# VectorE computes one of the four exponential banks in 88 of 1024 units of an attention layer

## The reference

```python
x = x + attn(_layernorm(x))          # in: (4, 2048, 256)
x = x + ffn(_layernorm(x))
# attn
qkv = einsum('bse,fe->bsf', x, in_proj_weight) + in_proj_bias
scores = einsum('bhqd,bhkd->bhqk', q * scale, k)
scores = where((j <= i) & (j >= i - 16), -inf, scores)
ctx = einsum('bhqk,bhkd->bhqd', softmax(scores), v)
out = einsum('bse,fe->bsf', ctx, out_proj_weight) + out_proj_bias
# ffn
h = tanh(((x @ weight) @ aux_weight1) @ aux_weight2 + bias)
```

## Time and profile before

| | us |
|---|---|
| median of 3 runs (2016.45 to 2018.87) | 2017.15 |
| the profiled execution's own time | 2016.49 |
| its span, first to last instruction | 2014.8 |
| ACT busy | 1927.0 (96%) |
| PE busy | 1822.5 (90%) |
| DVE busy | 703.0 (35%) |
| POOL busy | 153.7 (8%) |

### The profile page before, as it was taken

How to read it: one execution, slowest core, us unless ns; L and a number is a source line. 1 busy time by engine, 2 the same in 40 slices (tenths; PEclk the granted TensorE clock), 3 DMA queues, 4 the chain that set the end, 5 groups by cost and what they waited for, 6 DMA issues and landing times.

```text
span 2014.8 us, 100136 instructions
## 1 busy us (share of the span) xinstructions
PE 1822.5 (90%) x46728; PEld 752.1 (37%) x46728; DVE 703.0 (35%) x1415; ACT 1927.0 (96%) x2113; POOL 153.7 (8%) x178
## 2 busy tenths in 40 slices
PE   7799999999999999999999999999998978888895
PEld 4333343343434334343343434334342323223232
DVE  6233343433444343343434334343432212121123
ACT  4599999999999999999999999999999999999994
POOL 2000000101010010101101000010100000000001
PEclk9899999999999999999999999999999999999998
DMA  4400111101231110102221111211022010000101
GB/s 132 140 26 27 47 33 55 42 22 47 65 93 33 53 43 17 58 25 64 63 63 52 28 57 30 59 38 42 21 67 66 22 42 22 25 30 12 42 14 44
DMA packets 93448, 93.76 MB, mean 47 GB/s; under 512 B 17562, under 2 KB 84570, under 8 KB 93026
## 3 DMA queue, kind: packets, MB, share of 16 engines
q1 hardware_dynamic: 92772, 87.05, 14.8%
q10 hardware_dynamic: 256, 0.26, 0.1%
HBM read 52.56 MB, written 25.72 MB: 39 GB/s over the span
## 4 chain that ended last, share of the span: by engine, by line
ACT 54%; issue 29%; PE 15%; DMA 1%; DVE 1%; SPq 1%; POOL 0%; DVEq 0%
ACT probs L1220 53%; PE outs L1287 7%; PE scores L1268 4%; PE ps_qk L487 2%; ACT s_pre L1212 1%; PE ps_v L504 1%; PE spare L1370 1%; SPq L155 0%; PE spare L1315 0%; PE spare L1326 0%; PE ps_turn L457 0%; DMA inverse<-row_inverse 0%; DMA xin<-in_x 0%; PE spare L1302 0%; PE scores L1475 0%
## 5 line engine op out<-in xcount | busy, mean ns | idle before, releaser
L1220 ACT ACTIVATE probs<-scores 128x1024 f32<-128x1024 f32 x2048 | 1887.3, 1112 | 22.5 <-PE scores L1268 20.4
L1287 PE MATMUL outs<-probs,vs 64*32 64x512 f32 x16384 | 1077.1, 590 | 0.0
L1268 PE MATMUL scores<-qs,ks 49*32 49x512 f16 x16384 | 840.2, 383 | 158.8 <-ACT probs L1220 143.8
L1268 PEld LDWEIGHTS scores<-qs,ks 49*32 49x32 f16 x16384 | 233.8, 89 | 1079.2 <-ACT probs L1220 1044.2
L1287 PEld LDWEIGHTS outs<-probs,vs 64*32 64x32 f32 x16384 | 302.3, 106 | 35.7 <-issue 10.5
L886 DVE TENSOR_TENSOR probs<-probs,allowed 128x320 f32<-128x320 f32 (+2 forms) x280 | 147.5, 530 | 337.6 <-ACT probs L1220 337.4
L1326 PE MATMUL spare<-s_xt,w_qkv 64*32 64x256 f32 x3072 | 120.7, 375 | 0.0
L828 POOL TENSOR_TENSOR s_squares<-s_qk_f 128x512 bf16<-128x512 f32 x48 | 61.3, 1278 | 384.5 <-DVE s_qk_f L957 384.5
L822 POOL TENSOR_TENSOR s_x<-s_x,bias_o 128x1024 f32<-128x1024 f32 x16 | 38.2, 2385 | 573.7 <-DMA s_x<-in_x 573.7
L954 DVE TENSOR_SCALAR s_qk_f<-spare,bias_qk 128x512 f32<-128x512 f32 x48 | 36.1, 751 | 129.8 <-PE spare L1326 129.8
L1016 DVE TENSOR_TENSOR s_x<-s_x,spare 128x512 f32<-128x512 f32 x30 | 20.7, 688 | 171.5 <-PE spare L1326 171.5
(11 more groups left out here) (119 smaller groups left out, 786.6 us busy)
## 6 DMA issues: line engine op xcount, KB each, us to landing
qs<-q_parts SPq DMA_DIRECT2D x192, 64.0 KB
ks<-k_parts SPq DMA_DIRECT2D x192, 64.0 KB
inverse<-row_inverse SPq DMA_DIRECT2D x32, 256.0 KB
s_x<-in_x SPq DMA_DIRECT2D x16, 512.0 KB, 5.6
ctx_in<-raw SPq DMA_DIRECT2D x248, 32.0 KB, 2.0
out<-s_pre SPq DMA_DIRECT2D x15, 512.0 KB, 3.5
s_xin<-in_x SPq DMA_DIRECT2D x12, 512.0 KB, 6.3
q_parts<-s_parts SPq DMA_DIRECT2D x24, 256.0 KB, 2.3
```

Source lines behind the costliest of these rows:

```text
L1220: act.activation(probs[:, u % RING, 2 * slot:2 * slot + 2].rearrange("p c q -> p (c q)"), scores[:, 2 * slot:2 * slot + 2].rearrange("p c ...
L1268: last = pe.matmul(scores[cols, 2 * slot + e], ks[rows, group, keys], qs[rows, group], start=True, stop=True)
L1287: last = pe.matmul(outs[32 * c:32 * c + 32, side], vs[keys, at:at + 2 * HD], probs[keys, u % RING, c], start=(i == 0), stop=(i == KBLOCKS ...
```

## The change

In 88 units, ACT computes only three of the four banks (slot 1 becomes one instruction of 512 columns), and DVE computes `exp` of the fourth bank (bank 3) with a polynomial: `share(u, stage)`, in four stages at the positions u + 1 to u + 4. Stage 1 reads the bank from PSUM and signals `taken`, after which PE may write the bank again; the last instruction of stage 4 writes `probs` and signals `shared_done`. The units are r = 11, 27, 32, 42, 60 in steps 0 to 11, and r = 1, 7, 12, 27, 33, 38, 57 in steps 12 to 15. The weighing lags by a constant 5 units (before: 4 for i = 4 to 12 of a pass, 3 for i = 14 to 31 and the first three, two weighings at i = 13, none at i = 3). The ring has 7 units. At the position after a shared unit the weighing is cut into two halves of 256 columns, one on each side of `score(u, 1)`. Some pieces are moved by a position, `evacuate` goes from r = 3 and 35 to 5 and 37, `invert` from r = 8 and 40 to 10 and 42, and the fp16 high part of a projected query or key moves from `take_qk` to `split_low`, a position later.

```diff
-RING = 8
+RING = 7
+LAG = 5
-TURN_AT = (7, 8, 9, 10)
-QK_AT = ((12, 14, 15, 16), (18, 19, 20, 21), (33, 34, 35, 36), (38, 39, 40, 41))
+TURN_AT = (8, 9, 10, 11)
+QK_AT = ((13, 14, 15, 16), (18, 19, 20, 21), (33, 34, 35, 36), (39, 40, 41, 42))
...
-SQUASH_AT = {True: 72, False: 58}
+SQUASH_AT = {True: 73, False: 58}
+SHARED_AT = {True: (11, 27, 32, 42, 60), False: (1, 7, 12, 27, 33, 38, 57)}
...
+            def share(u, stage):
+                whole_bits = e_whole[:].bitcast(I32)
+                if stage == 1:
+                    dve.wait_ge(scored, 2 * u + 2)
+                    dve.tensor_scalar(e_arg[:], scores[:, HG - 1], LEAST, LOG2E, ALU.max, ALU.mult).then_inc(taken, 1)
+                    dve.wait_ge(taken, SHARED_BEFORE[u + 1])
+                    finished(dve.tensor_scalar(e_whole[:], e_arg[:], ROUND, None, ALU.add))
+                if stage == 2:
+                    finished(dve.scalar_tensor_tensor(out=e_rest[:], in0=e_whole[:], scalar=ROUND,
+                                                      in1=e_arg[:], op0=ALU.subtract, op1=ALU.subtract))
+                    dve.tensor_scalar(whole_bits, whole_bits, 23, None, ALU.logical_shift_left)
+                    finished(dve.tensor_scalar(e_arg[:], e_rest[:], POWER[5], None, ALU.mult))
+                for power in {3: (4, 3, 2), 4: (1,)}.get(stage, ()):
+                    finished(dve.scalar_tensor_tensor(out=e_arg[:], in0=e_arg[:], scalar=POWER[power], in1=e_rest[:],
+                                                      op0=ALU.add, op1=ALU.mult))
+                if stage == 4:
+                    if u >= RING:
+                        dve.wait_ge(summed, u - RING + 1)
+                    dve.scalar_tensor_tensor(out=probs[:, u % RING, HG - 1], in0=e_arg[:], scalar=POWER[0], in1=e_whole[:],
+                                             op0=ALU.add, op1=ALU.mult).then_inc(shared_done, 1)
...
+                if slot and is_shared(u - 1):
+                    pe.wait_ge(taken, SHARED_BEFORE[u])
...
+                if is_shared(u):
+                    pe.wait_ge(shared_done, SHARED_BEFORE[u + 1])
...
                     score(u, 0)
-                    due = weighed_at(u)
-                    if due:
-                        weigh(due[0])
-                    score(u, 1)
-                    for w in due[1:]:
-                        weigh(w)
+                    if due is None:
+                        score(u, 1)
+                    elif r % KBLOCKS == LAG:
+                        score(u, 1)
+                        weigh(due)
+                    elif is_shared(u - 1):
+                        weigh(due, 0, EMB)
+                        score(u, 1)
+                        weigh(due, EMB, CHUNK)
+                    else:
+                        weigh(due)
+                        score(u, 1)
```

More of the change, by code:

```diff
@@ L304, in set_ones @@
                 pool.memset(lay["vs"][buffer][:, KBLOCKS * V_ROW:], 1.0).then_inc(cleared, 1)
-                pool.wait_ge(cleared, count + 2)
+                pool.wait_ge(cleared, done + 2)
             rsqrt(0)
@@ L588, in stream @@
         pool_steps = count(1)
+        taken = sem("taken")
+        shared_done = sem("shared_done")
         scored = sem("scored")
@@ L670, in weighed_at, with is_shared @@
         def weighed_at(position):
[L673 to L684, removed]
-            return [u for u in found if 0 <= u < NCH * STEP]
+            return position - LAG if 0 <= position - LAG < NCH * STEP else None
+        def is_shared(u):
+            step, r = divmod(u, STEP)
+            return 0 <= step < NCH and r in SHARED_AT[step < PROJECTED]
+        SHARED_BEFORE = [sum(is_shared(v) for v in range(u)) for u in range(NCH * STEP + 1)]
         def finishing(step, r):
@@ L1078, in run_step @@
                         mask(seen)
+                    here = step * STEP + r
+                    if is_shared(here - 1):
+                        share(here - 1, 1)
                     for c, at, beside in finishing(step, r):
@@ L1138, in run_step @@
                             f_normalise(f, r - 38)
+                    for stage in (2, 3, 4):
+                        if is_shared(here - stage):
+                            share(here - stage, stage)
             dve.memset(sums_fine[:], 1.0).then_inc(fine_set, 1)
@@ L1219, in _ @@
                         act.wait_ge(summed, u - RING + 1)
-                    act.activation(probs[:, u % RING, 2 * slot:2 * slot + 2].rearrange("p c q -> p (c q)"),
-                                   scores[:, 2 * slot:2 * slot + 2].rearrange("p c q -> p (c q)"),
+                    banks = slice(2 * slot, HG - 1 if slot and is_shared(u) else 2 * slot + 2)
+                    act.activation(probs[:, u % RING, banks].rearrange("p c q -> p (c q)"),
+                                   scores[:, banks].rearrange("p c q -> p (c q)"),
                                    ACT.Exp, scale=1.0 / (SCALE_UP * SCALE_UP)).then_inc(exped, 1)
@@ L1286, in weigh @@
                         keys = slice(side * HALF_P, (side + 1) * HALF_P)
-                        last = pe.matmul(outs[32 * c:32 * c + 32, side], vs[keys, at:at + 2 * HD],
-                                         probs[keys, u % RING, c], start=(i == 0), stop=(i == KBLOCKS - 1))
-                last.then_inc(summed, 1)
+                        last = pe.matmul(outs[32 * c:32 * c + 32, side, lo:hi], vs[keys, at:at + 2 * HD],
+                                         probs[keys, u % RING, c, lo:hi], start=(i == 0),
+                                         stop=(i == KBLOCKS - 1))
+                if hi == CHUNK:
+                    last.then_inc(summed, 1)
             def fold_ffn(stage):
```

61 lines of the change are left out of this document (35 added, 26 removed).

## The result

The changed kernel takes **2061.03 us** (median of four runs, 2058.53 to 2066.46), the kernel before 2018.01 us beside it (2016.45 to 2020.57). The ratio is 1.0213, 95% interval 1.0199 to 1.0228: +43.0 us. The prediction was 2058 us. The profiled run took 2059.97 us.

What follows compares the result with a forecast made beforehand. ACT was taken as the bound, one exponential every 0.92 us. Terms -15 + 2 + 1 + 24 + 23.5 + 2.6 + 1 + 1.7 = +40.8 on 2014.8 gave a span of 2055.6, median 2058 us; range 2030 to 2071.

Steps and rivals of the forecast that it cites:

- ACT is the bound, and whatever makes a weighing late stops it for as long: Whole kernel: ACT busy 1927.0 of 2014.8 us; in slot 1 nothing is left, so a late weighing stops ACT equally long.
- A shared unit lasts 1.67 us and not 1.40, -15 us: At 88 shared units: next first scores stay 1.67 us behind slot 0's start, so each saves 0.17 us, not 0.44.
- What I expected to see: In shared units: exp(u + 1, 0) starts 1.67 us after exp(u, 0), with some 0.25 us of ACT idle.
- r = 42, 3.30 us between the stages, 1.98 late, +24 us: Unit 42: `take_qk` and `split_low` take 3.30 us against an allowance of 1.32, late by 1.98 us in 12 steps.
- r = 11, POOL's addition stops DVE, 2.13 late in 11 steps, +23.5 us: Unit 11: `copy_turned` leaves 0.07 us of allowance; POOL's 2.39 us `add_bias` stops the polynomial, 2.13 us late in 11 steps.
- The rule of the Trainium skill: DVE and POOL at SBUF: the shared port pair is an exclusive lock, so r = 11 loses 2.1 us a step.
- sharing at half speed: DVE beside POOL: alternative to the lock; L966 would take 1.1 us, not 1.41, and r = 11 lose 1.2 a step.
- r = 32 and r = 60, +3 us: `evacuate` behind r = 32 late by 0.19 us (+2), r = 60 late by 0.08 after `statistics` (+1), each in 11 steps.
- Steps 12 to 15, +2.6 and +1: Units r = 1, 33, 38 late by some 0.1, 0.2, 0.3 us, 0.65 a step; POOL's bias hits r = 12 in step 12.
- The tail, +1.7 us: End of kernel: five units left to weigh after the last scores instead of three, +1.7 us.
- The moves give nothing, bound -5: Longer lag gives masks more time, but ACT has only 22.5 us of idle: counted as nothing, bound -5 us.
- The half weighings: Beside shared units: 8 matmuls of 256 columns twice, hidden while PE waits for ACT; counted as nothing.

Runs made afterwards that it cites:

- Without the polynomial: Changed kernel in which nobody computes the fourth bank of the 88 units, and weighings take what the ring held: 1998.53 us, 2015.55 before.
- two experiments: Changed kernel with the fourth bank computed by nobody (1998.53 us, 2015.55 before), and changed kernel with no unit shared (2015.05 us, 2017.83 before).
- the run: Changed kernel with empty lists of shared units, keeping the lag of 5, the ring of 7 and the moved pieces: 2015.05 us, 2017.83 before.
- the bias after the polynomial: Changed kernel in which POOL's bias addition waits for the polynomial of r = 11 (r = 12 in steps 12 to 15): 2033.46 us, 2015.55 before.
- both after: Changed kernel with POOL's bias addition behind r = 11's polynomial, and `split_low` and POOL's square behind r = 42's: 2007.38 us, 2017.83 before.

## Why the prediction was right, step by step

- *ACT is the bound, and whatever makes a weighing late stops it for as long*: right. PE waits 40.3 us for `probs`, and ACT has 59.6 us of new idle time (I had said some 80). Without the polynomial the time is 17.0 us below before, with it 43.0 above, so it costs 60.0 us. Against that kernel, whose exponentials have 28.1 us of idle time before them, the changed one has 54.0 more: the waits are most of the cost. ACT's idle time is longer than PE's waits in part because the clock fell behind some of them (last section).
- *A shared unit lasts 1.67 us and not 1.40, -15 us*: right. 1.65 in the timeline, -14.2 us between two experiments. What I expected to see was wrong: not 0.25 us of idle time, since one exponential starts before the one ahead of it has ended. The short record is 0.70 us long (590.59 to 591.29), so only 0.05 us show as idle before 591.34. For the same reason the busy time of the exponentials fell by 19.2 us and not by 38: the short record is 0.43 us shorter than a full one (1.13), but the next exponential starts only 0.17 us sooner, since the 0.21 us by which a full one runs into the next is gone. Here one must read starts, not busy time.
- *r = 42, 3.30 us between the stages, 1.98 late, +24 us*: the size is exact. 3.30 us between stage 1 and stage 2, a gap of 1.98 or 1.99 in five of ten steps, and 1.95 on the mean; times 12 it is 23.4. The kernel with `split_low` moved shows the cause: with 1.79 of the 3.30 us gone, so is the gap.
- *r = 11, POOL's addition stops DVE, 2.13 late in 11 steps, +23.5 us*: the mechanism is right, and the size a mixture. One instruction of the polynomial grew from 0.69 to 2.75 or more, and the gap of a step in which TensorE kept its clock is 1.78 on the mean (1.67 to 1.95 in steps 3, 4, 5, 9 and 10). In the other five of steps 2 to 11 it is 3.11 to 3.42, which I hadn't foreseen. The mean over the ten is 2.52.
- *The rule of the Trainium skill that this rests on*, in "SBUF — State Buffer", section "SBUF: two separate sides", that the port pair of VectorE and GpSimd is locked and the second one stands still: this trace agrees, and shows it in both directions. L1102 waits for L827 and is 2.06 us too long; and L827, which started 0.53 us before the last product ended (596.83 against 597.36), is itself 2.76 long, 0.37 more than the same addition in the kernel before. By the working of the prediction, sharing at half speed would have left 0.9 us less.
- *r = 32 and r = 60, +3 us*: too much. Where these units or the `evacuate` behind them would be late, at positions 37, 38, 65 and 66, ACT stands for 0.06 us a step or less. The gaps at positions 58 to 60 stand before unit 60 is weighed, and the kernel before has them too, so they are no part of this term.
- *Steps 12 to 15, +2.6 and +1*: the small latenesses are about right, and the place of POOL's addition is wrong. I had it at unit 12 in step 12 alone (a gap of 0.78 at position 17), but it hits unit 12 in steps 13 to 15 as well. This is step 13:

```profile
1660.25 40.81 ACT L1261 ACTIVATE probs<-scores 128x1024 f32<-128x1024 f32 x45
1701.82 47.14 ACT L1261 ACTIVATE probs<-scores 128x1024 f32<-128x1024 f32 x52 [0.75 <-PE scores L1311]
...
1696.45 2.60 POOL L827 TENSOR_TENSOR s_x<-s_x,bias_o 128x1024 f32<-128x1024 f32 x1 [80.17 <-DMA s_x<-in_x]
...
1700.46 1.09 PE L1332 MATMUL outs<-probs,vs 64*32 64x512 f32 x16 [0.77 <-DVE probs L1102]
```

  In these steps the tanh stands at position 58, so the first exponential behind it is that of unit 59, and 45 later it is the second one of position 17, where unit 12 is weighed. The addition starts 36 us after that first exponential (1660.25 to 1696.45), where I had read 6.9 to 9.4 us in steps with a projection. The three gaps that I had left out are 2.3 us; with those of 0.24 at position 43 all four steps have 0.98 to 1.02 us of gaps each.
- *The tail, +1.7 us*: right. The last exponential ends at 2023.67, and the copy of `outs` starts 3.19 us later, against 1.50 before:

```profile
2014.37 9.30 ACT L1261 ACTIVATE probs<-scores 128x1024 f32<-128x1024 f32 x10
...
2022.26 4.48 PE L1332 MATMUL outs<-probs,vs 64*32 64x512 f32 x80
...
2026.86 0.69 DVE L899 COPY raw<-outs 128x512 f32<-128x512 f32 x1 [7.55 <-PE outs L1332]
```

- *The moves give nothing, bound -5*: mis-sized, though inside the bound. With the tail in it the run shows -2.8, so the moves themselves gave 4.5. The half weighings too, costed at nothing, gave about 5.2 us of the 14.2.

The sum came out near because a gain that I left out (4.5 us of moves) stood against a loss that I left out (the clock, some 7 us: five steps of 3.26 on the mean against 1.78). So do the terms for r = 32 and 60, some 2 us too large, and for steps 12 to 15, some 1 us too small. That these nearly cancel is luck; the mechanisms of the two large terms and of the short exponential are not.

## What to carry to other kernels

When an engine that is nearly free takes over work, its average load says little; count for each piece how long it may take before the engine at the bound asks for it, and what stands in its own queue in between. Both losses here were cured without giving up a single shared unit, by moving a neighbour for which no compute engine waited. If two engines must not use SBUF at the same time, tie the one that has time to the end of the other.

## What the runs showed that I had not expected

**A wait of PE can cost twice.** The windows of the changed kernel give the busy times of PE, PEld, DVE, ACT and POOL in each stretch, then the granted TensorE clock and the DMA share. I took ten stretches of 4 us at position 16, one in each of steps 2 to 11; those of steps 2, 3 and 8:

```profile
352.30:356.30 4.00, 3.39 (x55) 2.55 (x63) 0.60 (x2) 0.83 (x2) 0.00 (x0) 0.62 0.02 4
475.50:479.50 4.00, 2.38 (x65) 1.30 (x64) 2.12 (x4) 2.40 (x3) 0.40 (x1) 1.00 0.02 4
...
1090.00:1094.00 4.00, 3.42 (x52) 1.80 (x60) 0.52 (x2) 0.99 (x1) 0.00 (x0) 0.57 0.04 11
```

Of the ten, five have a clock of 0.57 to 0.67, and they are just the five whose gaps come to more than 3 us; the other five have 1.00. In step 8 the weighing behind the wait and the exponential behind it look like this:

```profile
1090.58 1.96 PE L1332 MATMUL outs<-probs,vs 64*32 64x512 f32 x16 [1.96 <-DVE probs L1102]
...
1093.01 1.03 ACT L1261 ACTIVATE probs<-scores 128x1024 f32<-128x1024 f32 x1 [3.02 <-PE scores L1311]
```

The weighing takes 1.96 us, where it takes 1.09 in step 4 (at 600.28): from 2.4 GHz the clock went to 1.2 (0.51 in the stretch from 1092 to 1094 us) and came back. PE had waited 1.96 us before it; but at 659.07 it had waited 2.00 us, and kept 1.00. What decides between the two outcomes is open. It needs no second late polynomial. Here is the bias after the polynomial, around position 47 of step 5, where only unit 42 is late and the gaps come to 3.5 us:

```profile
772.00:774.00 2.00, 1.70 (x34) 1.32 (x41) 0.75 (x2) 0.00 (x0) 0.00 (x0) 0.79 0.05 12
774.00:776.00 2.00, 2.00 (x55) 1.63 (x47) 0.79 (x2) 1.43 (x2) 0.00 (x0) 0.50 0.00 0
```

Of steps 1 to 11, this happens in five with both units late (all at position 16), in three with the bias moved and in two with unit 11 not shared (at position 47), in two with `split_low` moved (at position 16), and in none with unit 42 not shared or with both after. That is one profiled run of each, so whether one late unit makes a fall at the other more likely isn't shown. It is part of why taking out unit 42's wait gave back more than its own share: in those two kernels the falls at position 16 went from five to none and two.

**POOL also slows an instruction with one input.** In step 4 of the kernel with `split_low` moved, its first part (an instruction with one input from SBUF) took 1.26 us beside POOL's square (651.63 to 652.96), instead of 0.43:

```profile
650.77 0.69 DVE L1104 SCALAR_TENSOR_TENSOR probs<-p_arg,p_whole 128x512 f32<-128x512 f32 x1
651.98 1.26 DVE L971 TENSOR_SCALAR s_parts<-s_qk_f 128x512 f16<-128x512 f32 x1
```

The changed kernel has it too: 24 of its 48 L969 start 0.2 us after the square and take 1.26 or 1.27 us. Those that start just before the square keep 0.43.
